# Mixture-of-experts tiles: transposing the experts' rows by VectorE in 32x32 blocks, with a rearranging load, in place of TensorE

## What is computed

```python
x = x + tanh(g_xattn) * xattn(layernorm(x), ctx, mask, Wq, Wk, Wv, Wo)
x = x + tanh(g_ffn) * ffn(layernorm(x), Wg, W1, W2, W3)

def ffn(x, Wg, W1, W2, W3):          # D = 256, H = 512, E = 8, K = 2
    top_v, top_i = top_k(einsum('bsd,ed->bse', x, Wg), 2)
    probs = softmax(top_v)
    for e in range(8):
        w_e = sum(probs * (top_i == e))
        g = silu(x @ W1[e].T) * (x @ W2[e].T)
        out = out + (g @ W3[e].T) * w_e
```

## Time and profile before

| what | us |
|---|---|
| runs | 665.76, 661.04, 665.11 (median 665.11) |
| the profiled execution | 661.78 |
| its span, first to last instruction | 660.0 |

### The profile page before, as it was taken

How to read it: one execution, slowest core, us unless ns; L and a number is a source line. 1 busy time by engine, 2 the same in 40 slices (tenths; PEclk the granted TensorE clock), 3 DMA queues, 4 the chain that set the end, 5 groups by cost and what they waited for, 6 DMA issues and landing times.

```text
span 660.0 us, 10752 instructions
## 1 busy us (share of the span) xinstructions
PE 622.1 (94%) x2958; PEld 346.2 (52%) x2959; DVE 393.6 (60%) x1187; ACT 287.7 (44%) x744; POOL 309.2 (47%) x272
## 2 busy tenths in 40 slices
PE   4599999999999999999999999699999999999994
PEld 2244445454555544455554555256666666666663
DVE  3767788888987878988769977333251212221211
ACT  1556665656555564564545554023322222222221
POOL 2345565555564587564685564502464222222221
PEclk9989999999999999999999998899999999999998
DMA  8904577676766776757677569969556322333221
GB/s 273 333 1 104 144 168 170 142 167 146 163 149 150 161 186 163 166 130 184 134 193 179 135 158 249 269 186 377 161 142 131 49 41 42 47 48 48 46 23 22
DMA packets 92652, 95.37 MB, mean 144 GB/s; under 512 B 11056, under 2 KB 86704, under 8 KB 92592
## 3 DMA queue, kind: packets, MB, share of 16 engines
q1 hardware_dynamic: 69968, 71.64, 41.9%
q10 hardware_dynamic: 15840, 14.07, 9.4%
q0 software_dynamic: 6784, 8.95, 8.2%
HBM read 27.72 MB, written 12.36 MB: 61 GB/s over the span
## 4 chain that ended last, share of the span: by engine, by line
PE 77%; POOL 6%; DMA 5%; issue 4%; DVE 4%; ACT 2%; ACTq 1%; POOLq 0%; SPq 0%; DVEq 0%
PE ps_s L1396 17%; PE ps_s L1216 14%; PE ps_o L1241 13%; PE ps_o L1424 8%; PE ps_a L1149 7%; PE ps_a L1251 7%; POOL probs L525 3%; POOL x_regrouped L513 2%; DMA out_dram<-yg,ids 2%; PE ps_o L1227 2%; PE ps_t L1417 2%; PE ps_s L1143 2%; DVE blocksT L996 2%; DMA probsT<-blocksT 1%; DMA wk_sb<-Wk_dram 1%
## 5 line engine op out<-in xcount | busy, mean ns | idle before, releaser
L525 POOL TENSOR_TENSOR probs<-probs,inv_sum 128x802 f32<-128x802 f32 x128 | 194.8, 1524 | 154.5 <-DVE inv_sum L975 153.7
L636 ACT ACTIVATE probs<-probs,neg_max 128x401 f32<-128x401 f32 x256 | 159.3, 624 | 147.1 <-DVE neg_max L984 147.0
L984 DVE CUSTOM_DVE_ANT_0 probs<-ps_s,biases 128x401 f32<-128x401 f32 x256 | 136.9, 573 | 52.5 <-PE ps_s L1216 51.6
L1396 PE MATMUL ps_s<-w_sb,xgT 128*128 x296 | 139.5, 594 | 1.4 <-ACT xgT L732 1.4
L996 DVE STREAM_TRANSPOSE blocksT<-probs 128x832 f32<-128x832 f32 x128 | 133.2, 1040 | 9.0 <-POOL probs L525 9.0
L564 POOL DMA_INDIRECT out_dram<-yg,ids x36 | 56.0, 1555 | 159.4 <-DVE yg L1108 136.5
L1241 PE MATMUL ps_o<-probsT,v_sb 128*64 128x512 f32 x512 | 125.0, 612 | 4.4 <-DMA probsT<-blocksT 4.4
L1216 PEld LDWEIGHTS ps_s<-kT,qT 64*128 64x128 f32 x1024 | 82.9, 187 | 78.6 <-DVE neg_max L984 42.2
L1216 PE MATMUL ps_s<-kT,qT 64*128 64x201 f32 (+1 forms) x1024 | 122.0, 357 | 1.4 <-issue 1.4
L1096 DVE TENSOR_TENSOR gated<-ps_s,silu 128x512 f32<-128x512 f32 x37 | 25.6, 692 | 117.5 <-PE ps_s L1396 112.1
L1396 PEld LDWEIGHTS ps_s<-w_sb,xgT 128*128 128x128 f32 x296 | 53.0, 191 | 39.5 <-issue 37.9
(11 more groups left out here) (142 smaller groups left out, 420.9 us busy)
## 6 DMA issues: line engine op xcount, KB each, us to landing
probsT<-blocksT SPq DMA_DIRECT2D x285, 96.0 KB
probsT<-blocksT SPq DMA_DIRECT2D x95, 128.0 KB
probsT<-blocksT ACTq DMA_DIRECT2D x99, 96.0 KB
xg<-x_regrouped SPq DMA_DIRECT2D x39, 129.0 KB, 2.1
probsT<-blocksT ACTq DMA_DIRECT2D x33, 128.0 KB
w_sb<-W1T_dram SPq DMA_DIRECT2D x8, 512.0 KB, 9.5
w_sb<-W2T_dram SPq DMA_DIRECT2D x8, 512.0 KB, 10.2
w_sb<-W3T_dram SPq DMA_DIRECT2D x8, 512.0 KB, 10.5
```

What stands on the lines that cost most here:

```text
L525: pool.tensor_tensor(duo, duo, inv_sum[:, u:u + 2].unsqueeze(2).to_broadcast([P, 2, LASTK]), ALU.mult)\
L636: act.activation(probs[:, b, 0:LASTK], probs[:, b, 0:LASTK], ACT.Exp, bias=neg_max[:, b:b + 1], scale=-1.0, accum_out=sum_exp[:, b:b + 1]) ...
L984: dve.tensor_tensor_reduce(probs[:, b, 0:LASTK], ps_s[u % 4][:, 0:LASTK], biases[:, tile, :], HD ** -0.5, 3e38, ALU.add, ALU.min, neg_max[ ...
L1396: mm = pe.matmul(bank[:, :], xgT[:, buf, k, :], w_sb[:, bass.ds(expert, 1), (n * KT + k) * FH:(n * KT + k + 1) * FH].squeeze(1), start=(k ...
```

## The change

TensorE no longer transposes the experts' rows, and ScalarE no longer copies them out of PSUM. `load_tile` moves a tile with five DMAs in place of one: four bring quarters of 64 features, so that the rows of partition group q hold feature quarter q of rows j, 32+j, 64+j and 96+j, and a fifth brings the weight and the row number to `xw`. VectorE then transposes 32x32 blocks with one instruction per tile, straight to `xgT`, now a ring of four, three tiles ahead. So that features land where the weights expect them, `rows` are written in a permuted order of features, and the gate weights are laid out to match. The order on SyncE's queue changes: expert 1's weights come after the wait for the last regrouping DMAs, only tiles 0 to 2 are loaded before expert 2, tile 3 after expert 2, and tiles 4 to 7 one each ahead of experts 4 to 7. VectorE runs the transposes of tiles 0 to 2 ahead of `gate(0)`, and that of tile s+3 at the end of tile s.

```diff
             def load_tile(i, k):
                 row = table(sp, 0, s, NOWHERE)
-                sp.dma_start(xg[:, k % RING, :], x_regrouped[bass.ds(row, P), :]).then_inc(xg_in[k % RING], 16)
+                tile = x_regrouped[bass.ds(row, P), :]
+                for q in range(4):
+                    sp.dma_start(xg_blocks[32 * q:32 * q + 32, k % RING, :, :],
+                                 tile[:, q * D // 4:(q + 1) * D // 4].rearrange("(b j) n -> j b n", j=32))\
+                      .then_inc(xg_in[k % RING], 16)
+                sp.dma_start(xw[:, k % RING, :], tile[:, D:]).then_inc(xg_in[k % RING], 16)
...
-                load_expert(sp, 1)
                 expert_there(0)
                 for slot in range(2):
                     sp.wait_ge(probsT_in[slot], 16 * REGROUP * CHUNKS // 2)
+                load_expert(sp, 1)
                 sp.wait_ge(sched_ready, 2)
                 sp.wait_ge(scattered, 16 * 2 * GT * (NR - 1))
-                for k in range(RING):
+                for k in range(3):
                     load_tile(0, k)
                 sp.wait_ge(masked_ready, 2 * DUOS)
                 load_expert(sp, 2)
+                load_tile(0, 3)
                 load_expert(sp, 3)
                 expert_there(1)
                 sp.wait_ge(pv_ready, CHUNKS)
                 for e in range(4, NE):
+                    load_tile(0, e)
                     load_expert(sp, e)
                     expert_there(e - 2)
...
-            def copy_xgT(s, buf):
-                act.wait_ge(xgT_ps, s + 1)
-                act.copy(xgT[:, buf, :, :], ps_t[1][:, 0:KT * P].rearrange("p (k n) -> p k n", k=KT))\
-                   .then_inc(xgT_ready, 1)
...
+            def transpose_x(i, k):
+                dve.wait_ge(xg_in[k % RING], 16 * 5 * (i + k // RING + 1))
+                dve.transpose(xgT[:, k % 4, :, :].rearrange("p h (b j) -> p b h j", j=32),
+                              xg_blocks[:, k % RING, :, :].rearrange("p b (h i) -> p b h i", i=32)).then_inc(xgT_ready, 1)
...
             def ffn_tile(i, k):
                     gate(s + 1)
                 weigh(i, k)
+                if not (isinstance(s, int) and s + 3 >= NG):
+                    transpose_x(i, k + 3)
             dve.sem_inc(y_ready, 1)
+            for k in range(3):
+                transpose_x(0, k)
             gate(0)
...
-                for c in range(KT):
-                    mm = pe.transpose(ps_t[1][:, c * P:(c + 1) * P], xg[:, k % RING, c * P:(c + 1) * P], ident[:, :])
-                mm.then_inc(xgT_ps, 1)
...
-                if not (last and s + 2 >= NG):
-                    transpose_x(i, k + 2)
                 project_down(s, now)
...
-        "WgT": a["L0_ffn_Wg"].T,
+        "WgT": a["L0_ffn_Wg"].T.reshape(2, 4, 32, 8).transpose(1, 0, 2, 3).reshape(256, 8),
```

More of the change, by code:

```diff
@@ L185, in build @@
             w_sb = sb("w_sb", [P, NE, EW], F32, ffn)
-            xgT = sb("xgT", [P, 2, KT, P], F32, ffn)
+            xgT = sb("xgT", [P, 4, KT, P], F32, ffn)
             silu = sb("silu", [P, FH], F32, ffn)
-            to_blocks = sb("to_blocks", [P, 272], F32, ffn)
-            xg = sb("xg", [P, RING, XW], F32, ffn)
+            xg_blocks = sb("xg_blocks", [P, RING, 4, D // 4], F32, ffn)
+            xw = sb("xw", [P, RING, XW - D], F32, ffn)
             ids = sb("ids", [P, RING], I32, ffn)
@@ L247, in build @@
         xg_in = [sem(f"xg{n}_in") for n in range(RING)]
-        xgT_ps, xgT_ready = sem("xgT_ps"), sem("xgT_ready")
+        xgT_ready = sem("xgT_ready")
         h1_ps, h2_ps, silu_ready, gated_ready = sem("h1_ps"), sem("h2_ps"), sem("silu_ready"), sem("gated_ready")
@@ L430, in _ @@
             for s in range(FULL, NG):
-                sp.wait_ge(xg_in[s % RING], 16 * (s // RING + 1))
+                sp.wait_ge(xg_in[s % RING], 16 * 5 * (s // RING + 1))
                 with sp.If(there > s):
@@ L751, in ffn_tile @@
                     silu_of(s + 1)
-                if not (isinstance(s, int) and s + 2 >= NG):
-                    copy_xgT(s + 2, k % 2)
             act.sem_inc(gatedT_ready, 1)
-            copy_xgT(0, 0)
             silu_of(0)
-            copy_xgT(1, 1)
             for n in range(N1):
@@ L889, in routing @@
                     for t in (2 * s - 12, 2 * s - 11):
-                        dve.tensor_scalar(rows[:, 0, t, 0:D], xs[:, bass.ds(GT * r + t, 1), :].squeeze(1),
+                        row = rows[:, 0, t, 0:D].rearrange("p (q h i) -> p h q i", q=4, h=KT)
+                        dve.tensor_scalar(row, xs[:, bass.ds(GT * r + t, 1), :].squeeze(1).rearrange("p (h q i) -> p h q i", h=KT, q=4),
                                           r_mean_var[:, t, 0:1], var[:, 0, t:t + 1], ALU.subtract, ALU.mult)\
@@ L1096, in gate @@
                 dve.tensor_tensor(gated[:, :], ps_s[1][:, :], silu[:, :], ALU.mult).then_inc(gated_ready, 1)
+            def transpose_x(i, k):
+                dve.wait_ge(xg_in[k % RING], 16 * 5 * (i + k // RING + 1))
+                dve.transpose(xgT[:, k % 4, :, :].rearrange("p h (b j) -> p b h j", j=32),
+                              xg_blocks[:, k % RING, :, :].rearrange("p b (h i) -> p b h i", i=32)).then_inc(xgT_ready, 1)
             def weigh(i, k):
                 s = RING * i + k
-                dve.wait_ge(xg_in[k % RING], 16 * (i + k // RING + 1))
                 if not first(s, RING):
                     dve.wait_ge(added, 16 * (s - RING + 1))
-                dve.tensor_copy(ids[:, k % RING:k % RING + 1], xg[:, k % RING, ID_COL:]).then_inc(ids_ready, 1)
+                dve.tensor_copy(ids[:, k % RING:k % RING + 1], xw[:, k % RING, ID_COL - D:]).then_inc(ids_ready, 1)
                 dve.wait_ge(y_ps, s + 2)
@@ L1107, in weigh @@
                     dve.wait_ge(added, 16 * (s - 1))
-                dve.tensor_scalar(yg[:, k % 2, :], ps_o[:, 0:D], xg[:, k % RING, W_COL:W_COL + 1], None, ALU.mult)\
+                dve.tensor_scalar(yg[:, k % 2, :], ps_o[:, 0:D], xw[:, k % RING, W_COL - D:W_COL - D + 1], None, ALU.mult)\
                    .then_inc(y_ready, 1)
@@ L1428, in _ @@
             pe.wait_ge(sched_ready, 2)
-            transpose_x(0, 0)
             expert = table(pe, 1, 0, NE - 1)
@@ L1432, in _ @@
             second_hidden(0, 0, expert)
-            transpose_x(0, 1)
             def ffn_tile(i, k):
@@ L1439, in ffn_tile @@
                     ahead = table(pe, 1, s + 1, NE - 1)
-                    first_hidden(s + 1, (k + 1) % 2, ahead)
+                    first_hidden(s + 1, (k + 1) % 4, ahead)
                 transpose_gated(s)
                 if not (last and s + 1 >= NG):
-                    second_hidden(s + 1, (k + 1) % 2, ahead)
+                    second_hidden(s + 1, (k + 1) % 4, ahead)
                 now = table(pe, 1, s, NE - 1)
-                if not (last and s + 2 >= NG):
-                    transpose_x(i, k + 2)
                 project_down(s, now)
```

## The result

| what | before | after |
|---|---|---|
| median of 20 runs each, us | 665.01 (661.04 to 668.36) | 661.09 (658.99 to 664.31) |
| ratio to before, 95% interval | | 0.9949 (0.9930 to 0.9967) |
| profiled execution, its span | 661.78, 660.0 | 659.74, 658.0 |

What follows compares the result with a forecast made beforehand. TensorE alone was taken to bound the tile stage, 5.83 us per steady tile. 661.8 - 7.9 + 0.2 + 0 = 654.1 us for the profiled execution, 657.4 on the median's scale; range 651.5 to 664.

Steps and rivals of the forecast that it cites:

- What goes: Tile stage: TensorE's row transposes leave the chain, 0.22 us in each of 36 tiles, 7.9 us saved.
- VectorE's part: Tile stage: a block transpose takes 0.32 us, at most 1.04, inside VectorE's 3.4 us idle before `gate`, at no cost.
- SyncE's part: Tile loading: 0.54 us per quarter, 3.4 us per tile (2.9 to 4.0), hidden in steady tiles, may show in two places.
- rival 5: Tile loading: SyncE becomes the bound at 7.1 us a tile, slower, about 690 us; chance 0.08.
- Small packets: Tile loads: a tile's 256 B and 8 B packets take 1.2 us of all engines, between 0.5 and 2.4.
- Rival 3: Tile loads: 256 B packets cost what 1032 B ones cost, 2.4 us a tile, tiles 8 and 2 late, 660.8 us; chance 0.13.
- The experts' weights: Weights and tiles in one queue: weights end about 473 (469.5 to 479), tile 8 has 3.3 us slack; term 0.
- The handover: Attention to experts: tile 0 transposed at 433.5, tile 2's landing sets `transpose_gated(0)` near 440; term +0.2 us (-1.2 to +4.9).
- rival 2: Handover free: tile 2 early, TensorE sets the pace, 9.1 us gained, 656.0 us; chance 0.15.
- rival 1: Handover gives the gain back through late scatters and slow issues: 3.0 us gained, 662.1 us; chance 0.22.
- Rival 4: After the handover: a granted clock below 1.00 after 430, costing 1.7 us; chance 0.05.

Runs made afterwards that it cites:

- e4: Changed kernel with two unused TensorE transposes of constant data per tile put back; ratio to the kernel before 1.0059, 667.21 us.
- e9: Changed kernel with tile 0's transpose before the attention branch's end and one tile loaded ahead of nearly every expert's weights; ratio to the kernel before 0.9898.
- e10: e9 with `gate(0)` ahead of the transpose of tile 2 on VectorE; ratio to the kernel before 0.9915.
- e13: e9 with tile 8 requested ahead of the last expert's weights; ratio to the kernel before 0.9883.
- e1: Changed kernel with VectorE's transpose of tile 0 moved before the end of the attention branch; ratio to the kernel before 0.9883, 656.46 us.
- e11: Repeat of e1, unaltered; ratio to the kernel before 0.9870.
- e2: Changed kernel with expert 1's weights requested after tiles 0 to 2; ratio to the kernel before 0.9941.
- e12: The changed kernel itself, unedited, run again beside e11; ratio to the kernel before 0.9956.
- e14: e13 with tile 0's transpose behind the attention branch again, same queue order; ratio to the kernel before 0.9939.
- e7: e1 with three constant matmuls into an unused bank on TensorE ahead of W1 of tile 0; ratio to the kernel before 0.9898.
- e8: Changed kernel, tile 0's transpose before the branch's end, tiles 0 to 3 ahead of experts 1 and 2, two constant matmuls before W1; ratio to before 0.9908.
- e5: Kernel before with only expert 1's weights moved behind the wait for the last regrouping DMAs; ratio to the kernel before 1.0008.

## Why the prediction was half right

**What goes: right.** 36 x 0.22 = 7.9 us were forecast; T to end fell by 7.7, a steady tile takes 5.60 us, and e4 puts 7.3 back. The rule of the Trainium skill (*VectorE: DVE Perf Modes*, "Rules for kernel authors") that the prediction weighed would have kept the work on TensorE; the load that rearranges quarters makes a whole transpose of VectorE's blocks, and the saving came as the rows had it.

**VectorE's part: right, one size off.** A block transpose takes 0.435 us, not 0.32 in proportion, within the bounds. `gate` still waits 33.1 us in 11 tiles, 3.0 each where 3.0 was forecast, so it costs nothing.

**SyncE's part: right, but for the first tiles.** Issues and landing of the quarters by line (duration ns min/median/max):

```profile
L356 SPq DMA_DIRECT2D xg_blocks<-x_regrouped x156: 316/317/1429, 428.4 to 624.2; - x156
...
DMA to landing us min/median/max: 1.6/1.8/4.5
```

The DMA instruction of a quarter takes what a plain load's takes, 0.32. With the work on its address a quarter takes 0.51 us (four from 476.74 to 478.79), and it was this sum that the forecast put at 0.54. Two successive tiles behind the weights start at 476.74 and 479.93, 3.2 us apart (3.4 forecast). In the handover tiles 0 to 2 start 3.57 and 4.21 us apart, the second above the bound of 4.0, as one issue took 1.43 us. The first quarter went out at 428.44 in a kernel that was 1.6 us late in attention; 427.8 was forecast. Of rival 5 nothing is seen.

**Small packets: between the bounds, cheaper than taken.** DMA packets of q1 from 432 to 438.5 us (packets, MB, share of 16 engines), in the changed kernel and then in the kernel before:

```profile
q1 hardware_dynamic: 1670, 0.36, 29.6%
```

```profile
q1 hardware_dynamic: 729, 0.67, 43.2%
```

0.296 x 16 x 6.5 us / 1670 is 18 ns a packet, as a mean of four of 256 B and one of 8 B, so one of 256 B took at most 18 x 5 / 4 = 23 ns; in the kernel before, with packets of 1032 B, it is 62 ns. The 640 packets of a tile make 640 x 18 / 16 = 0.7 us of all engines, where I took 1.2 between 0.5 and 2.4. Rival 3 is out. The Trainium skill (*DMA: Bandwidth & Descriptors*, "Specifications") puts line rate at 512 B and more. The trace agrees in part: for the same bytes the small packets took 1.3 times as long (30.8 us of an engine for 0.36 MB against 44.9 us for 0.67 MB), far from the 4 times of rival 3. Whether a read-modify-write is behind it no row here shows.

**The experts' weights: right.** The DMA share falls from 0.65 in 470 to 475 us to 0.38 in the next 5, so the weights ended about 475 (473 forecast, 479 at most), and tile 8 was transposed at 481.81 without a wait. In e9 and e10, where it kept VectorE waiting for 5.3 and 5.5 us, TensorE was idle for 2.0 and 1.4 us.

**The handover: the step that failed.** The sentence was "VectorE has its last residual until 433.13; tile 0 is transposed at 433.5". It took VectorE to be ready as soon as its last instruction of attention had ended. In fact it issues nothing for 3.1 us behind the branch, and the term of +0.2 us was +4.1. Its parts by e13: without the gap W to T is 10.57, 0.6 less than before, so rival 2 was on its way; the exposed gap adds 3.2 to TensorE's idle time (4.87 - 1.63) and the clock 1.5 (6.92 - 5.41). That is -0.6 + 3.2 + 1.5 = +4.1, and 7.7 - 4.1 = 3.6.

Three more things in that step were off. Its own sum, 439.0 + 0.35 + 0.7, gives 440.05 and not 440.2, a term of 0.0; that changes little. Tile 0 was not there at 432 but at 434.6, 0.1 us ahead of the end of the residual (434.7), as its DMAs took 3.7 to 4.3 us to land; that path has no slack left, and in the profiles of e1 and e11 it was the longer one. And tile 2's landing set nothing. It was transposed at 440.69 after 1.6 us of waiting, but `gate(0)` then waited 2.98 us more for TensorE. Nearest in time was rival 1 (662.1), but by another mechanism: the wait for the scatters was 0.4 us and tile 0 had landed before VectorE was ready. That 661.1 lies in the range at all is owed to the bounds of that rival, so it is luck. Rival 4 had the mechanism of the second part and nearly its size, 1.7 us for 1.5, and got a chance of 0.05, since the two gaps of the kernel before, 0.66 and 0.75 us, had done no harm. It hung on the gap that I had not seen. Its sign, a granted clock below 1.00 after 430, came.

The rows to see it were there. VectorE had no instruction between 433.13 and 437.20, and I put all of that down to `gate` waiting for TensorE. The queue's own first instruction behind the branch, at 436.5, said when VectorE could have started.

## What to carry to other kernels

When work moves to an engine that was idle, read whether it was free to issue, not only that it was not busy: look at its queue's next instruction, above all behind a branch or between two programs of a kernel. An idle stretch ahead of a wait can hide a gap that becomes the critical path as soon as something is due in it, and if TensorE is idle through it, a lower clock can add to the bill, here 1.5 to 2.8 us to the gap's 3.2. The remedy was to issue the first operation on the near side of the branch, and to check in one list which load is last before each is due.

## What the runs showed of the hardware

- Behind the end of the attention branch VectorE issued nothing for 3.0 to 3.2 us (after, e2, e4, e12, e14; counted from the end of its last work there 3.1 to 3.4, and 3.4 in the kernel before). TensorE issued nothing behind its own for 1.4 us (e7), 1.1 (e8) and 0.9 (e5), and had no such gap in the kernel before.
- Idle times of TensorE of 4.4 to 4.9 us were followed by a stretch at a lower granted clock in each of seven profiles, 1.63 us in none of five; the price was 1.5 to 2.8 us.
- DMA packets, four of 256 B to one of 8 B, took 18 ns of an engine each where packets of 1032 B took 62, which is 1.3 times as long for the same bytes. A quarter tile over 32 partitions was issued in 0.32 us, like a whole one over 128 (0.33).
- A block transpose of 128x256 float32 took 0.435 us, one of 128x832 1.04. A line through these two shapes, as an estimate, is 0.17 us and 1.05 ns per element of a partition.
